# Pair stage of a graph network: ScalarE builds four of every seven batches of the targets' one-hots, and the ring of one-hot buffers grows from three to four

## The reference

```python
src, dst = (edge_index[0], edge_index[1])
msg = x[src]
agg = jax.ops.segment_sum(msg, dst, num_segments=N)
deg = jax.ops.segment_sum(jnp.ones((src.shape[0],), x.dtype), dst, num_segments=N)
mean = agg / jnp.maximum(deg, 1.0)[:, None]
h = relu(mean @ W1n + b1n + x @ W1r + (x @ Wl1 + bl1))     # the second half of the layer and layers 2 to 4 follow
```

## Time and profile before

| | |
|---|---|
| median of 3 runs (lowest, highest) | 3910.35 us (3905.66, 3910.69) |
| the profiled execution, its own time | 3914.72 us |
| its span, first to last instruction | 3913.0 us |
| mean granted TensorE clock, of full | 0.915 |
| PE / DVE / ACT / POOL busy, share of the span | 78% / 83% / 55% / 34% |
| pair stage, 600 to 800 us: PE / DVE / ACT busy | 89% / 97% / 36% |

### The profile page before, as it was taken

How to read it: one execution, slowest core, us unless ns; L and a number is a source line. 1 busy time by engine, 2 the same in 40 slices (tenths; PEclk the granted TensorE clock), 3 DMA queues, 4 the chain that set the end, 5 groups by cost and what they waited for, 6 DMA issues and landing times.

```text
span 3913.0 us, 125366 instructions
## 1 busy us (share of the span) xinstructions
PE 3052.9 (78%) x50473; PEld 2725.6 (70%) x50473; DVE 3231.2 (83%) x6988; ACT 2164.1 (55%) x5734; POOL 1346.9 (34%) x1644
## 2 busy tenths in 40 slices
PE   0288888888888779899677778777757778788786
PEld 0167777777777679899677777777746777777775
DVE  7599999999999733233899999999967889989997
ACT  5323333333333410001778878788756888888887
POOL 2000000000000000000487778778753555555554
PEclk9999999999999989999899999999877888888887
DMA  8156666666666779898676777777628888888884
GB/s 210 54 168 205 209 206 209 208 209 208 212 213 211 233 297 361 342 327 301 229 245 225 236 236 243 224 241 241 229 92 273 256 251 256 257 258 255 253 255 141
DMA packets 655939, 907.64 MB, mean 232 GB/s; under 512 B 363978, under 2 KB 587883, under 8 KB 636412
## 3 DMA queue, kind: packets, MB, share of 16 engines
q1 hardware_dynamic: 633240, 800.64, 63.7%
q10 hardware_dynamic: 19763, 94.38, 6.4%
q0 software_dynamic: 2352, 4.52, 0.6%
HBM read 651.96 MB, written 247.40 MB: 230 GB/s over the span
## 4 chain that ended last, share of the span: by engine, by line
DVE 39%; PE 30%; DMA 11%; ACT 9%; issue 7%; SPq 2%; POOL 1%; ACTq 0%; DVEq 0%; POOLq 0%
PE ps L626 7%; PE ps L964 7%; DVE U L754 5%; DMA U<-AD 3%; DMA A<-ROWS 3%; DVE EDG L777 3%; DMA T<-ROWS 3%; DVE U L1271 2%; PE ps L1178 2%; DVE EDG L1300 2%; PE ps L1190 2%; PE ps L1171 2%; DVE U L1632 2%; DVE U L1263 2%; SPq L1396 2%
## 5 line engine op out<-in xcount | busy, mean ns | idle before, releaser
L542 ACT ACTIVATE U<-ps 128x512 bf16<-128x512 f32 (+1 forms) x637 | 359.1, 573 | 666.3 <-PE ps L638 666.0
L1148 POOL TENSOR_TENSOR EDG<-U,edge 128x256 f32<-128x256 f32 x343 | 243.3, 710 | 852.5 <-DVE edge L1296 733.1
L1464 ACT ACTIVATE U<-U,T 128x65 f32<-128x65 f32 x1806 | 459.7, 339 | 107.5 <-PE ps L1552 94.2
L1178 PE MATMUL ps<-U 128*128 128x65 bf16 x7203 | 304.2, 200 | 209.3 <-DVE edge L1274 207.5
L964 PE MATMUL ps<-U 128*128 128x192 bf16 x4802 | 421.2, 249 | 37.6 <-DVE U L1041 19.2
L487 POOL DMA_INDIRECT U<-REC,nod x49 | 45.2, 922 | 1164.7 <-PE ps L582 1041.5
L964 PEld LDWEIGHTS ps<-U 128*128 128x128 bf16 x4802 | 405.7, 99 | 46.6 <-DMA U<-AD 23.2
L1178 PEld LDWEIGHTS ps<-U 128*128 128x128 bf16 x7203 | 265.6, 102 | 231.0 <-DVE edge L1274 228.6
L777 DVE TENSOR_TENSOR EDG<-edge,EDG 128x896 bf16<-128x896 bf16 x686 | 406.6, 618 | 8.9 <-DMA OSD<-EDG 7.5
L1490 POOL TENSOR_TENSOR U<-U 128x455 f32<-128x455 f32 x258 | 275.7, 1069 | 329.7 <-DVE U L1632 329.7
L651 PE MATMUL ps<-EDG,U 128*128 128x193 bf16 x2401 | 310.8, 251 | 62.5 <-ACT U L542 41.3
(11 more groups left out here) (303 smaller groups left out, 7407.2 us busy)
## 6 DMA issues: line engine op xcount, KB each, us to landing
U<-AD SPq DMA_DIRECT2D x98, 1568.0 KB, 8.6
U<-ROWS SPq DMA_DIRECT2D x343, 448.0 KB, 4.4
OND<-EDG SPq DMA_DIRECT2D x343, 224.0 KB, 2.3
OSD<-EDG SPq DMA_DIRECT2D x343, 224.0 KB, 3.2
AD<-U ACTq DMA_DIRECT2D x49, 1568.0 KB, 6.4
EDG<-ROWS SPq DMA_DIRECT2D x343, 224.0 KB, 4.9
U<-OND SPq DMA_DIRECT2D x303, 224.0 KB, 5.2
EDG<-OSD SPq DMA_DIRECT2D x189, 224.0 KB, 4.7
```

The source lines that it names most:

```text
L542: ev4.by(act.activation(prow[i % NPW][:, P * g:P * (g + m)], ps[4 + gg % 2][:, 0:P * m], ACT.Copy))
L1178: ins = pe.matmul(ps[2 + h][:, 65 * k:65 * k + 65], rw[r][:, 2 * P * k:2 * P * k + P], Ws[:, j, s_, 0:65], start=(s_ == 0), stop=(s_ == 2))
L1464: ins = act.activation(V4[k % NV][:, 0, c, :], H[d % 3][:, s, :], ACT.Copy, scale=a4[d % 2][:, s:s + 1])
```

## The change

In four of the seven batches, b = 1, 3, 5 and 6 (`BYA`), DVE makes only OS, and ACT makes OD. ACT has no compare, so it computes |v - c| and then relu(1 - |v - c|), which is 1 where the slot's position v equals the column c and 0 elsewhere, as all are whole numbers. v is a per-partition bias, so |v - c| takes one instruction of 128 x 128 per pair, seven per batch (L576 of the changed file), and one relu of 128 x 896 in place follows (L579). They are spread over three values of n: three |v - c| at n = 0, 3, 6, 9, two at n = 1, 4, 7, 10, and the last two with the relu at n = 2, 5, 8, 11. Within n they stand behind the evacuation of group n-2 and ahead of the dense layer's line. PE's `count` and SP's stores wait for a second semaphore, `hot_a`. The ring gets a fourth pair of buffers (`NHB = 4`), so a batch waits for batch k-4. The other edits rename a semaphore of a later stage and move a small helper up.

```diff
-        NHB = 3
+        NHB = 4
+        BYA = (1, 3, 5, 6)
...
+        def made_a(k):
+            return len(BYA) * (k // NH7) + sum(b <= k % NH7 for b in BYA)
...
                 sp.wait_ge(hot8.at, k + 1)
+                if b in BYA:
+                    sp.wait_ge(hot_a.at, hot_a.o + made_a(k))
...
+            def hots(i, n):
+                if n >= 3 * len(BYA):
+                    return
+                b = BYA[n // 3]
+                k = NH7 * i + b
+                r = k % NHB
+                if n % 3 == 0:
+                    act.wait_ge(slot_ev.at, i + 1)
+                    if k >= NHB:
+                        kk = k - NHB
+                        act.wait_ge(count4.at, NG4 * (kk // NH7) + (7 * (kk % NH7) + 6) // 4 + 1)
+                        act.wait_ge(hot_st[r].at, 32 * (k // NHB))
+                for c in ((0, 1, 2), (3, 4), (5, 6))[n % 3]:
+                    ac.by(act.activation(OD[r][:, c, :], iota1, ACT.Abs, scale=-1.0, bias=E3[:, i, 1, 7 * b + c:7 * b + c + 1]))
+                if n % 3 == 2:
+                    act.wait_ge(ac.at, ac.n)
+                    hot_a.by(act.activation(OD[r].rearrange("p c r -> p (c r)"), OD[r].rearrange("p c r -> p (c r)"), ACT.Relu, bias=1.0, scale=-1.0))
...
                     if i is not None and n >= 2:
                         count(i, n - 2)
+                    if i is not None:
+                        hots(i, n)
                     if d is not None:
                         dense(d, n)
...
                 pe.wait_ge(hot8.at, NH7 * i + (g + m - 1) // 7 + 1)
+                pe.wait_ge(hot_a.at, hot_a.o + made_a(NH7 * i + (g + m - 1) // 7))
...
-                for o_, s in ((OS, 0), (OD, 1)) if n == 0 else (((OS, 0),) if n % 2 else ((OD, 1),)):
-                    ins = dve.tensor_tensor(o_[r].rearrange("p c (r k) -> p c r k", k=2), bc(r1v.unsqueeze(1), [P, 7, D, 2]),
-                                            bc(sdb[i % 2][:, s, 7 * b:7 * b + 7, :].unsqueeze(2), [P, 7, D, 2]), ALU.is_equal)
-                    (dv if s == 0 else hot8).by(ins)
+                if n % 2 or n == 0:
+                    ins = dve.tensor_tensor(OS[r].rearrange("p c (r k) -> p c r k", k=2), bc(r1v.unsqueeze(1), [P, 7, D, 2]),
+                                            bc(sdb[i % 2][:, 0, 7 * b:7 * b + 7, :].unsqueeze(2), [P, 7, D, 2]), ALU.is_equal)
+                    (hot8 if b in BYA else dv).by(ins)
+                if n % 2 == 0 and b not in BYA:
+                    hot8.by(dve.tensor_tensor(OD[r].rearrange("p c (r k) -> p c r k", k=2), bc(r1v.unsqueeze(1), [P, 7, D, 2]),
+                                              bc(sdb[i % 2][:, 1, 7 * b:7 * b + 7, :].unsqueeze(2), [P, 7, D, 2]), ALU.is_equal))
```

More of the change, by code:

```diff
@@ L134, in part, with on @@
             return U[:, start:start + n]
+        def on(s, o):
+            return Sem(s.at, o)
         dv, ac = sem("dve_step"), sem("act_step")
@@ L434, in gnn_kernel @@
         Xs3 = Xs[:, :, 0:3 * D].rearrange("p b (s f) -> p b s f", s=3)
-        NHB = 3
+        NHB = 4
         NH7, GH = 7, 7 * P
-        OS = [EDG[:, 4730 + 448 * i:4730 + 448 * i + 448].bitcast(BF16).rearrange("p (c r) -> p c r", r=P) for i in range(NHB)]
-        OD = [EDG[:, 6074 + 448 * i:6074 + 448 * i + 448].bitcast(BF16).rearrange("p (c r) -> p c r", r=P) for i in range(NHB)]
+        spare = part(o2 + 6272, 896)
+        OS = [o.bitcast(BF16).rearrange("p (c r) -> p c r", r=P)
+              for o in [EDG[:, 4730 + 448 * i:4730 + 448 * i + 448] for i in range(NHB - 1)] + [spare[:, 0:448]]]
+        OD = [o.bitcast(BF16).rearrange("p (c r) -> p c r", r=P)
+              for o in [EDG[:, 6074 + 448 * i:6074 + 448 * i + 448] for i in range(NHB - 1)] + [spare[:, 448:896]]]
+        BYA = (1, 3, 5, 6)
         rst = [EDG[:, 7802 + P * i:7802 + P * i + P].bitcast(BF16) for i in range(2)]
@@ L456, in gnn_kernel @@
         rank_ok, fld_hot, slot_mm, slot_ev, slot_ea = sem("rank_ok"), sem("field_hot"), sem("slot_mm"), sem("slot_evac"), sem("slot_evac_act")
+        hot_a = on(cnt_mm, 1)
         hot8, count4, ev4 = sem("pair_hot"), sem("pair_count"), sem("pair_evac")
@@ L1089, in gnn_kernel @@
         rows_ld = [sem(f"rows_ld{i}") for i in range(NR)]
-        hot_a, hot_d = sem("ends_hot_act"), sem("ends_hot_dve")
+        hot_ea, hot_d = sem("ends_hot_act"), sem("ends_hot_dve")
         c_got, r_got, c_ev, r_used = sem("c_got"), sem("r_got"), sem("c_ev"), sem("r_used")
@@ L1093, in gnn_kernel @@
         os_ld = [sem(f"os_ld{i}") for i in range(4)]
-        def on(s, o):
-            return Sem(s.at, o)
         rem3, low3, rem3p = on(hid, NB), on(relu, NB), on(outp, NB)
@@ L1165, in ends @@
                 else:
-                    pe.wait_ge(hot_a.at, by_act(n))
+                    pe.wait_ge(hot_ea.at, by_act(n))
                 if n >= 2:
@@ L1212, in columns @@
                     act.wait_ge(ac.at, ac.n)
-                    hot_a.by(act.activation(rw[r], rw[r], ACT.Relu, bias=1.0, scale=-1.0))
+                    hot_ea.by(act.activation(rw[r], rw[r], ACT.Relu, bias=1.0, scale=-1.0))
             def ends(n):
@@ L1713, in gnn_kernel @@
         z_inc, z_carry, z_fix, z_agg, z_read = again(ln_i), again(ln_o), again(normed), again(pj_t), again(pj_ev)
-        z_cat, z_t, z_ct, z_h, z_r, z_o, z_x2 = again(pj_mm), again(pj_out), again(nr_i), again(nr_o), again(ws_i), again(ws_o), again(hot_a)
+        z_cat, z_t, z_ct, z_h, z_r, z_o, z_x2 = again(pj_mm), again(pj_out), again(nr_i), again(nr_o), again(ws_i), again(ws_o), again(hot_ea)
         z_tab, z_tabst = again(hot_d), again(c_got)
```

## The result

| | median of the runs | ratio, 95% interval | mid-stage step |
|---|---|---|---|
| before | 3908.0 us | | 23.97 us |
| changed | 4389.9 us | 1.123 (1.121 to 1.125) | 34.13 us |

Forecast were 4229 us, a range of 4090 to 4350, and a step of 30.5 us. The sign and the place were right; the loss was 482 us where 319 were forecast. The step is the distance of DVE's L772 (L735 before) in mid-stage: 18 of them start between 608.4 and 1188.7 us, 580.3 / 17 = 34.13.

The account below looks back on a forecast made before the run. The prediction took DVE as the bound before, with PE close behind, and PE's waits for ACT after the change. Hand-offs of 5.5 and clock of 1.0 us over 49 steps added 319 us: 4229 us, range 4090 to 4350.

Parts of the forecast that it names:

- ACT's prices: ACT's new instructions: |v - c| over 128 columns 0.39 us long, relu over 896 columns 0.95 us; 12.1 us a step.
- The order as the bound: PE and ACT in mid-stage: PE waits for ACT's late parts and evacuations, making the step 29.5 us, not 23.98.
- The walk's 29.5 us: One mid-stage step followed through PE, ACT and DVE with measured spacings: 29.5 us, +5.5, before any clock loss.
- I take 1.0: Clock term: PE's new long waits lower the clock ahead of `slots`, costing 1.0 us a step.
- both `slots` lose 1.5: Upper bound of the clock term: both `slots` of a step run partly at the lower clock, 3.0 us together.
- The sum: Whole kernel: 49 steps a block times (5.5 + 1.0) us, +319 us on the median, 4229 us.
- The rival of the low clock: Clock stays low for most of PE's work: 33.5 us a step, +467, 4377 us; chance 0.07.
- DVE stays the bound: Mid-stage: ACT's parts hide in its waits, DVE saves 2.16 us a step, 21.8 us, 3805 us; chance 0.03.

Follow-up runs that it names:

- with the clock held up: Changed kernel plus extra PE products whose results are overwritten: 36 ahead of the counts of groups 1 and 10, 20 ahead of the `cat_ev` wait; 4192.1 us.
- batches 1 and 6: Changed kernel with only these two batches' OD on ACT, in parts, and 36 extra PE products ahead of the counts of groups 1 and 10; 4052.5 us.
- three batches: Changed kernel, but ACT makes OD of batches 3, 4 (n = 4) and 6 (n = 9) whole, with the dense layer's lines first; 3919.1 us.
- the run with step 22.89: Changed kernel, but ACT makes only batches 3 and 6, whole, dense layer's lines first, and DVE's dense-layer input comes right behind the ranks; 3861.4 us.
- group 1's filled: Changed kernel with 36 extra PE products, results overwritten, ahead of the count of group 1 only; 4234.3 us.

## Why the prediction went wrong

- *ACT's prices* were right: 394 and 952 ns measured, 0.39 and 0.95 us worked out from an instruction of another width.
- *The order as the bound* was right. The walk's 29.5 us stand against 29.83 with the clock held up, and 26.7, walked in the same way before the run, against 26.84 for batches 1 and 6.
- *The step that failed is the clock's*: "I take 1.0", with "3.0 us (both `slots` lose 1.5)" as the upper bound. It measured 4.3. The bound counted only the two `slots`, and took what one case near the stage's end had lost as the most that one can lose. In the changed step the clock is low twice. The first low stretch covers the last `use`, `offsets` and the hand-over to `runs` (0.9 us: 19.28 for 18.24, less the 0.16 that were there before), the second two groups (0.3 us), the whole second `runs` (2.67 for 1.55) and much of the first `slots` (5.19 for 3.30). All of these are PE's on the path. So only one of the two `slots` lost anything, 1.9 us, while the other took its usual 3.44; the rest, over half of the 4.3, fell on work for which the bound had nothing. The reason given for the low value, that `runs` and three groups stand between the wait and `slots`, was turned the wrong way: they did not bring the clock back but ran slowly themselves (from 828 to 836 us PE is busy throughout, at a mean clock of 0.55).
- *The sum.* With 4.3 in place of 1.0 it is 49 x (5.5 + 4.3) = 480 us; 482 were measured. That the two agree so well is in part luck: the mid-stage step grew by 10.16 us, of which 49 would be 498, and the steps at the stage's two ends grew by less (the 48 distances between the first and the last L772 grew by 9.4 us on average).
- *The rival of the low clock*, 33.5 us a step and 4377 us, was the case that came, with 0.07. Its mechanism was in hand and the range stopped 27 us short of it.
- *The rival "DVE stays the bound", 3805 us*, was far off for this placing and was reached by none that was run. With three batches the step stays at 23.90 us while DVE waits 2.16 of it, so PE and its hand-offs take about as long as DVE there, where the text read only "PE is close behind". But its mechanism is the one of the run with step 22.89: two compares less on DVE, 1.08 us less a step. The text also read PE's waits as "only 0.39 us at a time". The same step of the kernel before has two longer ones, for an evacuation and for DVE's input of the dense layer; the second is the one that the run with step 22.89 took away:

```profile
713.64 0.51 PE L651 MATMUL ps<-EDG,U 128*128 128x193 bf16 x4 [0.83 <-ACT U L542]
...
720.87 0.33 PE L663 MATMUL ps<-ident,MISC 128*128 128x128 f32 x1 [0.66 <-DVE MISC L794]
```

## What to carry to other kernels

An engine with idle time is not free if the idle time is that of waiting for a partner. The placing that paid here put the new work in one piece in front of a wait known to be long; the same amount in small parts between the hand-offs, and of other batches, took 331 us more. Walk the order by hand with measured spacings; here this gave the step within 0.3 us in 30, with the clock held up. If the walk gives PE new waits of 2 us, let the upper bound have all that PE does behind them at 1.2 GHz, and not just its longest block.

## What was not expected of the hardware

- In the changed kernel the clock fell behind both waits of 2.16 and 2.30 us, and with group 1's filled even behind one of 1.21 us (four products of a group in 0.63 us from 809.35 on), which in the changed kernel it did not. The kernel before has waits of 0.4 to 0.8 us in mid-stage and stays at 1.00, and so does the run with step 22.89, which has one of 1.05.
- Work that nobody needs, 92 products of 128 columns a step, was free where PE waited and was worth 4390 - 4192 = 198 us by keeping the clock at 2.4 GHz.
- Filling one of two waits gains 3.4 or 2.8 us a step and both together 3.9: the clock's cost is not a sum over waits.
